# Attention scratch: sixteen heads' q and k scattered into a padded scratch and read back in two pieces

## The chip, the cores and the metric

One core of one Trainium2 chip runs the whole kernel. The metric is the device time of one execution in microseconds (us), the median of several runs.

## What is computed

The input `x` is (8, 256, 128) in float32: eight sequences of 256 tokens with 128 features. Two layers are applied, each the sum of an "attention" part and a "ffn" part on the normalised input:

```python
x = x + L0_attn(norm(x)) + L0_ffn(norm(x))
x = x + L1_attn(norm(x)) + L1_ffn(norm(x))
```

- `L0_attn` is an encoder block with 16 heads. The heads are cut by `reshape(B * 16, L, 8)`, without a transpose, so that head n of a sequence holds tokens 16 n to 16 n + 15, each with its 128 features seen as 16 rows of 8. `softmax(q k')` plus a relative position bias is multiplied by v; an output projection, a norm and a linear feed-forward follow.
- `L0_ffn` is a chain of six nodes, each with an 8-head attention of 16 features per head.
- `L1_attn` is a state space block (convolution, scan with 16 states, gated output) and a GELU feed-forward; `L1_ffn` routes each token to 2 of 8 experts.

## The kernel before, in words

The eight sequences are worked off one behind another in a software pipeline. Four lanes of stages (`CELL`, `SIDE`, `RAW`, `LAYER1`) exist for each sequence b; a table (`START`, `PLACES`) gives each stage of each engine a place, and every engine runs its stages in the order of these places, without reordering. So each engine is one queue in which work of up to three sequences is interleaved, and a stage that waits holds everything behind it on its engine. All DMAs are issued from one queue, that of SyncE (SP).

Attention B is the 8-head attention of the six nodes (groups 0 to 11 of four heads in each sequence); attention A is the 16-head one (groups 0 to 3). In both, q and k lie in strips of 32 partitions, four heads to a group: rows 0 to 15 (B) or 0 to 7 (A) of a strip are features, and row 16 (B) or 8 (A) holds -1 in k and the row maximum in q. A group goes through: `maximum` (L784, products q k' of the features alone), `tops` (L1307, row maxima on VectorE), `max_rows` (L792 transposes them on TensorE, ScalarE copies them at L1059, and SP sends them with a small DMA into the strips of q, L599), `score` (L802, the products again, now with the extra row, so that the maximum is subtracted), `exp` (L1066) and `values` (L815, L822).

For A, the projections give `qkv_a` (128 partitions, q, k and v of 256 tokens), with the features ordered so that a head must be gathered across tokens. That goes through a scratch in device memory:

- `a_write` (L566) writes q, k and v as they lie, 384 rows of 1 KB.
- `a_stack` (L585) reads the heads back with eight DMAs, one for q and one for k of each group. Each reads 4 heads x 512 rows in runs of 64 bytes, so that the strips come in with their 24 padding rows, for which the scratch has spare rows. It waits for `a_written` and for the last score of A of the sequence before.
- `v_read` (L592) reads v back in the same manner (16 heads x 128 rows of 64 bytes).
- `o_write`, `o_read` (L605, L611) take the attention's output back through a second scratch; L869 is the product that uses it.

In the SP queue, `a_write` and `a_stack` of sequence b stand ahead of `o_write` and of `rows B 10`, `o_read` and `rows B 11` of sequence b-1. For b = 0, 2 and 4 `a_stack` follows `a_write` at once; for the others `rows A 3` of the sequence before lies between them.

Of the kernel before, what the change touches and what calls it, by code (L numbers as in the profile page):

```python
# [7 lines left out]
F32 = mybir.dt.float32  # L8
# [173 lines left out]
def hybrid_layers(nc, t):  # L182

    ctx = ExitStack()
    with ctx:
        def sb(name, shape, dt=F32):
            return ctx.enter_context(nc.sbuf_tensor(name, shape, dt))
# [4 lines left out]
        def sig(name, per, step=1, sides=1):  # L192
            return Signal([one(f"{name}{i}" if sides > 1 else name) for i in range(sides)], per, step)
# [15 lines left out]
        rows = sb("rows", [P, t["rows"].shape[0], D])  # L209
# [35 lines left out]
        nt = sb("nt", [P, 2, NODES, L])  # L245
        qs = {"B": [sb(f"qs_b{i}", [P, 2, L]) for i in range(2)], "A": [sb(f"qs_a{i}", [P, L]) for i in range(A_GROUPS)]}
        ks = {"B": [sb(f"ks_b{i}", [P, 2, L]) for i in range(2)], "A": [sb(f"ks_a{i}", [P, L]) for i in range(A_GROUPS)]}
        qkv_a = sb("qkv_a", [P, 3, L])
# [108 lines left out]
        x_loaded = sig("x_loaded", 1, 16, 2)  # L357
        stacked_a = sig("stacked_a", 1, 2 * 4 * 16)
        maxed = {"B": [sig(f"maxed_B{i}", NODES, 16, 2) for i in range(2)], "A": [sig(f"maxed_A{i}", A_GROUPS // 2, 16) for i in range(2)]}
        a_written = sig("a_written", 1, 16)  # L360
        v_read = sig("v_read", 1, 16)
# [157 lines left out]
        def _(sp):  # L519
# [41 lines left out]
            def a_write(b):  # L561
                sp.wait_ge(*qkv_a_done.at(b, 1))
                hold(sp, s_held)
                past(sp, stacked_a, b - 1)
                past(sp, v_read, b - 1)
                sp.dma_start(bass.AP(tensor=a_scr.tensor, offset=0, ap=[[L, P], [A_PITCH * L, 3], [1, L]]), qkv_a[:, :, :]).then_inc(a_written.of(b), 16)  # L566
                if b == 0:
                    sp.wait_ge(s_memset, SETUP_POOL)
                    for first, n in A_SPARE:
                        sp.dma_start(a_scr[first:first + n, :], ks["A"][0][0:n, :]).then_inc(s_spare, 16)  # L570

            def gathered(i, first, heads, features):

                return bass.AP(tensor=a_scr.tensor, offset=i * A_PITCH * L + 16 * first, ap=[[16, heads], [L, 16 * features], [1, 16]])

            def a_stack(b):
                sp.wait_ge(*a_written.at(b))
                hold(sp, s_held)
                if b:
                    strips_ready(sp, b - 1, "score", "A", A_GROUPS - 1)  # L580
                else:
                    sp.wait_ge(s_spare, 16 * len(A_SPARE))
                for g in range(A_GROUPS):
                    for i, x in enumerate((qs["A"][g], ks["A"][g])):
                        sp.dma_start(x[:, :].rearrange("p (c r) -> p c r", c=CB), gathered(i, AG * g, AG, STRIP)).then_inc(stacked_a.of(b), 16)  # L585

            def v_read_(b):
                sp.wait_ge(*a_written.at(b))
                hold(sp, s_held)
                if b:  # L590
                    ready(sp, b - 1, "awo")
                sp.dma_start(va_hd[:, :].rearrange("p (c r) -> p c r", c=CB), gathered(2, 0, AH, AW)).then_inc(v_read.of(b), 16)  # L592

            def max_rows(b, kind, k):
                sp.wait_ge(*maxrow_done[kind].at(b, k))
                side, row = (b % 2, BW) if kind == "B" else (0, AW)
                x = qs["B"][side][:, k % 2, :] if kind == "B" else qs["A"][k][:, :]
                dst = bass.AP(tensor=x.tensor, offset=x.offset + row * x.ap[0][0], ap=[[STRIP * x.ap[0][0], 4], [1, L]])
                sp.dma_start(dst, maxrow[kind][side][k % 2][:, :]).then_inc(maxed[kind][k % 2].of(b), 16)  # L599
# [32 lines left out]
        def _(pe):  # L632
# [135 lines left out]

            def strip(tiles, b, kind, g, j, rows, first, n):
                part, span = slice(STRIP * j, STRIP * j + rows), slice(first, first + n)  # L770
                return tiles["B"][b % 2][part, g % 2, span] if kind == "B" else tiles["A"][g][part, span]

            def maximum(b, kind, g):
                if kind == "B":
                    pe.wait_ge(*k_done.at(b, g))
                    pe.wait_ge(*q_done.at(b, g))
                elif g == 0:
                    pe.wait_ge(*stacked_a.at(b))
                rows = BW if kind == "B" else AW
                take_strips(b, "max", kind, g)  # L780
                for qc in range(2):
                    for j in range(4):
                        o = strips[j // 2][:, (2 * (j % 2) + qc) * L:(2 * (j % 2) + qc + 1) * L]
                        mm = pe.matmul(o, strip(qs, b, kind, g, j, rows, qc * P, P), strip(ks, b, kind, g, j, rows, 0, L), start=True, stop=True)  # L784
                mm.then_inc(s_strips, 1)
# [9 lines left out]
            def score(b, kind, g):  # L795
                pe.wait_ge(*maxed[kind][g % 2].at(b, g // 2))
                rows = (BW if kind == "B" else AW) + 1
                take_strips(b, "score", kind, g)
                for kc in range(2):
                    for j in range(4):  # L800
                        o = strips[j // 2][:, (2 * (j % 2) + kc) * L:(2 * (j % 2) + kc + 1) * L]
                        mm = pe.matmul(o, strip(ks, b, kind, g, j, rows, kc * P, P), strip(qs, b, kind, g, j, rows, 0, L), start=True, stop=True)  # L802
                mm.then_inc(s_strips, 1)
# [745 lines left out]
        def _(pool):  # L1549
            pool.memset(half_neg[:, :], -0.5).then_inc(s_memset, 1)  # L1550
            pool.memset(vb[:, :, :, :, :], 0.0).then_inc(s_memset, 1)
            pool.memset(va[:, :, :, :], 0.0).then_inc(s_memset, 1)
            pool.memset(ks["A"][0][:, :], -1.0).then_inc(s_memset, 1)
            pool.memset(xi[:, :, :], 0.0).then_inc(s_memset, 1)
            pool.wait_ge(s_memset, 5)

# [82 lines left out]
SETUP_DVE = 3 * NODES + 2 * (NODES - 1) + 1 + 1 + 1 + 1 + 1 + CH + 2  # L1639
SETUP_POOL = 7  # L1640
T_BANK = (SETUP_DVE - 2) % 2
# [97 lines left out]
```

## Time and profile before

| | before |
|---|---|
| median of 3 runs | 1828.98 us (1828.89 to 1836.7) |
| profiled execution, its own time | 1828.94 us |
| its span, first to last instruction | 1827.1 us |
| busy: PE, DVE, ACT, POOL | 1384.5, 1066.4, 745.2, 271.6 us |
| mean granted TensorE clock | 0.808 |

PE is TensorE, DVE VectorE, ACT ScalarE, POOL GpSimd, and SPq the queue of SyncE. In a row of a timeline the first number is the start, the second the duration of the merged group, "xN" its count of instructions, and the bracket the engine's idle time just before it with what ended it. A float32 matmul is recorded as two instructions.

### The profile page before, as it was taken

How to read it: one execution, taken by the hardware profiler on the slowest of the kernel's cores; microseconds unless marked ns; L12 is line 12 of the kernel's file. 1: busy time of each engine (PE TensorE's matmuls, PEld its weight loads, DVE VectorE, ACT ScalarE, POOL GpSimd, SP SyncE). 2: the span in 40 equal slices, each digit the busy share in tenths (PEclk: the TensorE clock that was granted, in tenths of full speed). 3: DMA queues.
4: the chain of work that ended last, by engine and by line, in shares of the span. 5: the costliest groups of instructions: out<-in, count | busy, mean ns of one | idle time of the engine just before them, and what ended most of it. 6: DMA issues, size and time to landing. Idle time of an engine off the chain costs nothing.

```text
span 1827.1 us, 28722 instructions
## 1 busy us (share of the span) xinstructions
PE 1384.5 (76%) x10896; PEld 932.4 (51%) x10896; DVE 1066.4 (58%) x1757; ACT 745.2 (41%) x1420; POOL 271.6 (15%) x276
## 2 busy tenths in 40 slices
PE   6657866778598759876997959876987959778528
PEld 5434444445384437644664538544764538445407
DVE  2313323486368736784669536873668536875684
ACT  0223333455354534543455434542445434533323
POOL 0000001022111301031102201130102201121070
PEclk9667787779798879888897779867897779868858
DMA  4061021001210032002210131002110131001201
GB/s 154 23 62 12 2 29 16 1 13 21 45 62 4 22 53 56 13 13 35 57 39 13 17 49 62 5 21 35 48 39 12 18 48 59 4 13 42 83 1 61
DMA packets 199511, 62.20 MB, mean 34 GB/s; under 512 B 169232, under 2 KB 181296, under 8 KB 199248
## 3 DMA queue, kind: packets, MB, share of 16 engines
q1 hardware_dynamic: 199376, 60.36, 15.2%
q8 instruction: 90, 1.47, 0.3%
q14 instruction: 45, 0.37, 0.1%
HBM read 54.02 MB, written 5.80 MB: 33 GB/s over the span
## 4 chain that ended last, share of the span: by engine, by line
PE 51%; DVE 18%; SPq 14%; issue 7%; ACT 6%; DMA 3%; POOL 1%; DVEq 0%; ACTq 0%; POOLq 0%
SPq L585 12%; PE strips L802 9%; PE attn_out L815 7%; PE ps L963 6%; PE ps L975 5%; PE strips L784 5%; DVE hb L1448 4%; DVE rowmax_B L1307 3%; ACT probs L1066 3%; DVE hb L1443 2%; PE ps L740 2%; PE ps L644 2%; DVE rowmax_A L1307 2%; DVE work L1417 1%; PE attn_out L822 1%
## 5 line engine op out<-in xcount | busy, mean ns | idle before, releaser
L1066 ACT ACTIVATE probs<-strips 128x1024 f32<-128x1024 f32 x256 | 248.9, 1021 | 298.7 <-PE strips L802 298.0
L802 PE MATMUL strips<-qs_b,ks_b 17*128 17x256 f32 x1536 | 157.9, 541 | 203.6 <-DMA qs_b<-maxrow_B 139.8
L1307 DVE TENSOR_REDUCE rowmax_B<-strips 128x4 f32<-128x1024 f32 x192 | 227.2, 1219 | 136.0 <-PE strips L784 136.0
L802 PEld LDWEIGHTS strips<-qs_b,ks_b 17*128 17x128 f32 x1536 | 98.4, 255 | 241.7 <-DMA qs_b<-maxrow_B 142.3
L1448 DVE TENSOR_TENSOR_SCAN hb<-da,hb 128x1024 f32<-128x1024 f32 x64 | 149.2, 2331 | 2.2
L784 PE MATMUL strips<-ks_b,qs_b 16*128 16x256 f32 x1536 | 130.5, 460 | 22.8 <-ACT probs L1066 12.0
L815 PE MATMUL attn_out<-probs,vb 128*32 128x256 f32 x1536 | 142.2, 512 | 1.4 <-ACT probs L1066 1.4
L1534 DVE SCALAR_TENSOR_TENSOR work<-hb,ps 128x512 f32<-128x512 f32 x128 | 86.6, 686 | 96.2 <-ACT hb L1192 95.7
L975 PE MATMUL ps<-ze,w_e 128*128 128x256 f32 x512 | 127.2, 386 | 2.9 <-DVE work L1534 1.8
L963 PE MATMUL ps<-w_e,work 128*128 128x128 f32 x1024 | 125.1, 277 | 1.2 <-DVE work L1534 1.2
L963 PEld LDWEIGHTS ps<-w_e,work 128*128 128x128 f32 x1024 | 121.1, 192 | 8.2 <-DVE work L1534 4.5
L1153 ACT ACTIVATE da<-gate,a_neg 128x255 f32<-128x255 f32 x256 | 108.0, 496 | 21.0 <-DVE hb L1448 16.9
L784 PEld LDWEIGHTS strips<-ks_b,qs_b 16*128 16x128 f32 x1536 | 81.8, 216 | 64.7 <-issue 40.6
L1192 ACT ACTIVATE hb<-ps 128x512 f32<-128x512 f32 x128 | 75.5, 597 | 88.0 <-PE ps L975 85.9
L1618 POOL TENSOR_TENSOR cv_t<-hb 128x512 f32<-128x512 f32 x56 | 71.0, 1268 | 265.8 <-DVE hb L1452 265.8
L1074 ACT ACTIVATE out_sb<-attn_out 128x512 f32<-128x512 f32 x80 | 47.8, 597 | 148.7 <-PE attn_out L822 85.6
L975 PEld LDWEIGHTS ps<-ze,w_e 128*128 128x128 f32 x512 | 91.6, 190 | 22.1 <-issue 8.3
L1443 DVE TENSOR_TENSOR hb<-ps,dtx 128x1024 f32<-128x1024 f32 x64 | 78.0, 1218 | 38.0 <-PE ps L918 31.1
L1334 DVE TENSOR_TENSOR rem_a<-ps,xn_bo 128x256 f32<-128x256 f32 x8 | 3.4, 425 | 157.3 <-PE ps L869 157.3
L918 PE MATMUL ps<-bc,sel 96*128 96x256 bf16 x256 | 53.0, 328 | 53.1 <-DVE hb L1452 21.2
L815 PEld LDWEIGHTS attn_out<-probs,vb 128*32 128x32 f32 x1536 | 51.0, 137 | 73.0 <-issue 54.9
L1307 DVE TENSOR_REDUCE rowmax_A<-strips 128x4 f32<-128x1024 f32 x64 | 75.9, 1219 | 13.9 <-PE strips L784 13.9
(259 smaller groups left out, 2263.4 us busy)
## 6 DMA issues: line engine op xcount, KB each, us to landing
w_e<-in_w_e SPq DMA_DIRECT2D x128, 256.0 KB, 3.1
qs_a<-a_scr SPq DMA_DIRECT2D x32, 128.0 KB
ks_a<-a_scr SPq DMA_DIRECT2D x32, 128.0 KB
a_scr<-qkv_a SPq DMA_DIRECT2D x8, 384.0 KB, 2.6
pos<-t_scr SPq DMA_DIRECT2D x8, 264.0 KB, 11.3
qs_b<-maxrow_B SPq DMA_DIRECT2D x96, 4.0 KB
probs<-in_b_we_t SPq DMA_DIRECT2D x1, 1280.0 KB, 7.2
x_in<-in_x SPq DMA_DIRECT2D x8, 128.0 KB, 3.0
```

The costliest lines, as they stand in the source:

```text
L585: sp.dma_start(x[:, :].rearrange("p (c r) -> p c r", c=CB), gathered(i, AG * g, AG, STRIP)).then_inc(stacked_a.of(b), 16)
L784: mm = pe.matmul(o, strip(qs, b, kind, g, j, rows, qc * P, P), strip(ks, b, kind, g, j, rows, 0, L), start=True, stop=True)
L802: mm = pe.matmul(o, strip(ks, b, kind, g, j, rows, kc * P, P), strip(qs, b, kind, g, j, rows, 0, L), start=True, stop=True)
L815: mm = pe.matmul(attn_out[32 * j:32 * j + 32, i * L:(i + 1) * L], v, heads[:, j, kc, :], start=(kc == 0), stop=(kc == 1))
L963: mm = pe.matmul(o[:, h * D:(h + 1) * D], eh[:, e % 2, j, h * P:(h + 1) * P], w_e2[:, (b * EX + e) % RING, j, :], start=(j == 0), stop=(j ...
L975: mm = pe.matmul(o[:, j * L:(j + 1) * L], w_e1[:, n % RING, f * P:(f + 1) * P], ze[:, :], start=True, stop=True)
L1066: act.activation(probs[:, group % 2, 2 * i:2 * i + 2, :, :].rearrange("p h a b -> p (h a b)"), strips[i][:, :], ACT.Exp).then_inc(s_exp, 1)
L1153: last = act.activation(da[:, k % 2, m, j, 1:L], dt[:, m, 1:L], ACT.Exp, scale=a_neg[:, m, 2 * k + j:2 * k + j + 1])
L1307: dve.tensor_reduce(out=rowmax[kind][:, b % sides_n, k % 2, 2 * i:2 * i + 2, :], in_=strips[i][:, :].rearrange("p (h q t) -> p h q t", h=2 ...
L1443: dve.tensor_tensor(hk, o, dtx[:, :, :].unsqueeze(2).to_broadcast([P, CH, 2, L]), ALU.mult).then_inc(hb_done.of(b), 1)
L1448: dve.tensor_tensor_scan(flat_h, flat_a, flat_h, 0.0, ALU.mult, ALU.add).then_inc(scan_done.of(b), 1)
L1534: dve.scalar_tensor_tensor(out=eh[:, e % 2, 2 * k:2 * k + 2, :], in0=eh_t[:, i % 2, :, :], scalar=1.0, in1=parts_of(bank(b, ("h", i)), 2), ...
```

## The change

The scratch is laid out as the strips are: 32 heads' strips (16 of q, 16 of k) of 32 rows. It is filled with zeros once, and the rows of -1 are put in once. Per sequence, q and k are each scattered by one DMA in runs of 64 bytes (128 partitions x 16 heads), v goes to a scratch of its own, and the strips come back with one DMA for q and one for k, 512 rows of 1 KB each. `qs["A"]` and `ks["A"]` become one tile each for all four groups. The products of the strips take all 32 rows in place of 8, 9, 16 or 17. The setup has two memsets in place of one, and the fills of the scratch.

```diff
-A_PITCH = P + 16
-A_SPARE = [(P, 16), (A_PITCH + P, 16), (2 * A_PITCH + P, P), (2 * A_PITCH + 2 * P, A_PITCH + 16 * STRIP - 2 * A_PITCH - 2 * P)]
...
-        qs = {"B": [sb(f"qs_b{i}", [P, 2, L]) for i in range(2)], "A": [sb(f"qs_a{i}", [P, L]) for i in range(A_GROUPS)]}
+        qs = {"B": [sb(f"qs_b{i}", [P, 2, L]) for i in range(2)], "A": sb("qs_a", [P, A_GROUPS, L])}
...
-        a_scr = nc.dram_tensor("a_scr", [A_PITCH + 16 * STRIP, L], F32).ap()
+        a_scr = nc.dram_tensor("a_scr", [2 * AH * STRIP, L], F32).ap()
+        v_scr = nc.dram_tensor("v_scr", [P, AH, 16], F32).ap()
...
+            sp.wait_ge(s_memset, SETUP_POOL)
+            for i in range(2):
+                dst = bass.AP(tensor=a_scr.tensor, offset=i * AH * STRIP * L, ap=[[L, P], [P * L, A_GROUPS], [1, L]])
+                sp.dma_start(dst, ks["A"][:, :, :]).then_inc(s_spare, 16)
...
-                sp.dma_start(bass.AP(tensor=a_scr.tensor, offset=0, ap=[[L, P], [A_PITCH * L, 3], [1, L]]), qkv_a[:, :, :]).then_inc(a_written.of(b), 16)
                 if b == 0:
-                    sp.wait_ge(s_memset, SETUP_POOL)
-                    for first, n in A_SPARE:
-                        sp.dma_start(a_scr[first:first + n, :], ks["A"][0][0:n, :]).then_inc(s_spare, 16)
-
-            def gathered(i, first, heads, features):
-
-                return bass.AP(tensor=a_scr.tensor, offset=i * A_PITCH * L + 16 * first, ap=[[16, heads], [L, 16 * features], [1, 16]])
+                    sp.wait_ge(s_spare, 32)
+                    sp.dma_start(bass.AP(tensor=a_scr.tensor, offset=(AH * STRIP + AW) * L, ap=[[STRIP * L, AH], [1, L]]), qs["A"][0:AH, 0, :]).then_inc(s_spare, 16)
+                for i in range(2):
+                    dst = bass.AP(tensor=a_scr.tensor, offset=i * AH * STRIP * L, ap=[[16, P], [STRIP * L, AH], [1, 16]])
+                    sp.dma_start(dst, qkv_a[:, i, :].rearrange("p (n r) -> p n r", n=AH)).then_inc(a_written.of(b), 16)
+                sp.dma_start(v_scr.rearrange("p n r -> p (n r)"), qkv_a[:, 2, :]).then_inc(a_written.of(b), 16)
...
-                for g in range(A_GROUPS):
-                    for i, x in enumerate((qs["A"][g], ks["A"][g])):
-                        sp.dma_start(x[:, :].rearrange("p (c r) -> p c r", c=CB), gathered(i, AG * g, AG, STRIP)).then_inc(stacked_a.of(b), 16)
+                for i, x in enumerate((qs["A"], ks["A"])):
+                    src = bass.AP(tensor=a_scr.tensor, offset=i * AH * STRIP * L, ap=[[L, P], [P * L, A_GROUPS], [1, L]])
+                    sp.dma_start(x[:, :, :], src).then_inc(stacked_a.of(b), 16)
...
-                sp.dma_start(va_hd[:, :].rearrange("p (c r) -> p c r", c=CB), gathered(2, 0, AH, AW)).then_inc(v_read.of(b), 16)
+                src = bass.AP(tensor=v_scr.tensor, offset=0, ap=[[16, AH], [AH * 16, AW * CB], [1, 16]])
+                sp.dma_start(va_hd[:, :].rearrange("p (c r) -> p c r", c=CB), src).then_inc(v_read.of(b), 16)
...
-            def strip(tiles, b, kind, g, j, rows, first, n):
-                part, span = slice(STRIP * j, STRIP * j + rows), slice(first, first + n)
+            def strip(tiles, b, kind, g, j, first, n):
+                part, span = slice(STRIP * j, STRIP * j + STRIP), slice(first, first + n)
...
-            pool.memset(ks["A"][0][:, :], -1.0).then_inc(s_memset, 1)
+            pool.memset(ks["A"][:, :, :], 0.0).then_inc(s_memset, 1)
+            pool.memset(qs["A"][0:AH, 0, :], -1.0).then_inc(s_memset, 1)
```

## Rows read from the trace of the kernel before

**Rows 1.** The page's part 4: the chain that ended last, by line.

```profile
SPq L585 12%; PE strips L802 9%; PE attn_out L815 7%; PE ps L963 6%; PE ps L975 5%; PE strips L784 5%; DVE hb L1448 4%; DVE rowmax_B L1307 3%; ACT probs L1066 3%; DVE hb L1443 2%; PE ps L740 2%; PE ps L644 2%; DVE rowmax_A L1307 2%; DVE work L1417 1%; PE attn_out L822 1%
```

**Rows 2.** The page's part 5: busy time, mean, idle before, releaser.

```profile
L802 PE MATMUL strips<-qs_b,ks_b 17*128 17x256 f32 x1536 | 157.9, 541 | 203.6 <-DMA qs_b<-maxrow_B 139.8
```

**Rows 3.** Timeline of the SP queue around `a_stack` of sequence 4.

```profile
832.75 0.38 SPq L566 DMA_DIRECT2D a_scr<-qkv_a  x1
...
836.40 3.69 SPq L585 DMA_DIRECT2D ks_a<-a_scr  x1
...
863.29 3.70 SPq L605 DMA_DIRECT2D o_scr<-out_hd  x1
...
868.01 0.55 SPq L599 DMA_DIRECT2D qs_b<-maxrow_B  x1
868.67 0.37 SPq L611 DMA_DIRECT2D va_hd<-o_scr  x1
869.09 1.48 SPq L599 DMA_DIRECT2D qs_b<-maxrow_B  x1
```

**Rows 4.** Timeline of PE in the same stretch.

```profile
844.89 0.38 PE L792 MATMUL ps<-ident,rowmax_B 128*4 128x128 f32 x2 [0.35 <-DVE rowmax_B L1307]
...
852.27 0.38 PE L792 MATMUL ps<-ident,rowmax_B 128*4 128x128 f32 x2
870.78 2.09 PE L802 MATMUL strips<-qs_b,ks_b 17*128 17x256 f32 x16 [18.13 <-DMA qs_b<-maxrow_B]
```

**Rows 5.** PE timeline: the first of the eight such waits, sequence 0.

```profile
121.26 2.09 PE L802 MATMUL strips<-qs_b,ks_b 17*128 17x256 f32 x16 [12.43 <-DMA qs_b<-maxrow_B]
```

**Rows 6.** Timeline of ACT: the output of A copied for `o_write`.

```profile
845.08 0.38 ACT L1093 ACTIVATE out_hd<-ps 128x256 f32<-128x256 f32 x1
```

**Rows 7.** The last sequence, which no `a_stack` follows: SP, then PE.

```profile
1654.65 0.33 SPq L605 DMA_DIRECT2D o_scr<-out_hd  x1
...
1656.71 0.37 SPq L611 DMA_DIRECT2D va_hd<-o_scr  x1
...
1661.46 2.09 PE L802 MATMUL strips<-qs_b,ks_b 17*128 17x256 f32 x16
```

**Rows 8.** DMA issues: size of one, median us from issue to landing.

```profile
a_scr<-qkv_a SPq DMA_DIRECT2D x8, 384.0 KB, 2.6
...
va_hd<-o_scr SPq DMA_DIRECT2D x8, 128.0 KB, 3.6
```

**Rows 9.** SP timeline: `a_write` of sequence 7.

```profile
1431.39 0.38 SPq L566 DMA_DIRECT2D a_scr<-qkv_a  x1
...
1449.94 0.55 SPq L585 DMA_DIRECT2D qs_a<-a_scr  x1
```

**Rows 10.** Line L802: matmul durations in ns, shortest, median, longest.

```profile
L802 PE MATMUL strips<-qs_b,ks_b x1536: 374/626/792, 82.8 to 1667.2; 17*128 17x256 f32 x192
...
L802 PE MATMUL strips<-qs_a,ks_a x512: 374/374/791, 168.7 to 1645.3; 9*128 9x256 f32 x171
```

**Rows 11.** PE by stretch: us, busy (instructions), granted clock, DMA share, GB/s.

```profile
871.00:874.00 3.00, 3.00 (x20) 0.50 0.69 192
```

**Rows 12.** PE timeline: the same work for sequence 3 and for sequence 4.

```profile
811.98 2.04 PE L822 MATMUL attn_out<-pos,va 128*32 128x256 f32 x16
...
832.79 0.60 PE L833 MATMUL ps<-ident,out_sb 128*128 128x128 f32 x4
...
1009.68 1.94 PE L822 MATMUL attn_out<-pos,va 128*32 128x256 f32 x16
...
1037.36 0.60 PE L833 MATMUL ps<-ident,out_sb 128*128 128x128 f32 x4
```

**Rows 13.** PE timeline: scores of B before and after the wait of rows 4.

```profile
821.08 1.15 PE L802 MATMUL strips<-qs_b,ks_b 17*128 17x256 f32 x16 [0.38 <-ACT probs L1066]
...
824.36 1.15 PE L802 MATMUL strips<-qs_b,ks_b 17*128 17x256 f32 x16 [1.14 <-ACT probs L1066]
...
875.02 2.09 PE L802 MATMUL strips<-qs_b,ks_b 17*128 17x256 f32 x16 [1.00 <-ACT probs L1066]
```

More of the change, by code:

```diff
@@ L245, in hybrid_layers @@
         nt = sb("nt", [P, 2, NODES, L])
-        qs = {"B": [sb(f"qs_b{i}", [P, 2, L]) for i in range(2)], "A": [sb(f"qs_a{i}", [P, L]) for i in range(A_GROUPS)]}
-        ks = {"B": [sb(f"ks_b{i}", [P, 2, L]) for i in range(2)], "A": [sb(f"ks_a{i}", [P, L]) for i in range(A_GROUPS)]}
+        qs = {"B": [sb(f"qs_b{i}", [P, 2, L]) for i in range(2)], "A": sb("qs_a", [P, A_GROUPS, L])}
+        ks = {"B": [sb(f"ks_b{i}", [P, 2, L]) for i in range(2)], "A": sb("ks_a", [P, A_GROUPS, L])}
         qkv_a = sb("qkv_a", [P, 3, L])
@@ L357, in hybrid_layers @@
         x_loaded = sig("x_loaded", 1, 16, 2)
-        stacked_a = sig("stacked_a", 1, 2 * 4 * 16)
+        stacked_a = sig("stacked_a", 1, 2 * 16)
         maxed = {"B": [sig(f"maxed_B{i}", NODES, 16, 2) for i in range(2)], "A": [sig(f"maxed_A{i}", A_GROUPS // 2, 16) for i in range(2)]}
-        a_written = sig("a_written", 1, 16)
+        a_written = sig("a_written", 1, 3 * 16)
         v_read = sig("v_read", 1, 16)
@@ L581, in a_stack @@
                 else:
[L582 to L585 removed]
+                    sp.wait_ge(s_spare, 48)
+                for i, x in enumerate((qs["A"], ks["A"])):
+                    src = bass.AP(tensor=a_scr.tensor, offset=i * AH * STRIP * L, ap=[[L, P], [P * L, A_GROUPS], [1, L]])
+                    sp.dma_start(x[:, :, :], src).then_inc(stacked_a.of(b), 16)
             def v_read_(b):
@@ L596, in max_rows @@
                 side, row = (b % 2, BW) if kind == "B" else (0, AW)
-                x = qs["B"][side][:, k % 2, :] if kind == "B" else qs["A"][k][:, :]
+                x = qs["B"][side][:, k % 2, :] if kind == "B" else qs["A"][:, k, :]
                 dst = bass.AP(tensor=x.tensor, offset=x.offset + row * x.ap[0][0], ap=[[STRIP * x.ap[0][0], 4], [1, L]])
@@ L767, in take_strips @@
                             pe.wait_ge(s_exp, EXP_AT[user, kind, g, i] + 1)
-            def strip(tiles, b, kind, g, j, rows, first, n):
-                part, span = slice(STRIP * j, STRIP * j + rows), slice(first, first + n)
-                return tiles["B"][b % 2][part, g % 2, span] if kind == "B" else tiles["A"][g][part, span]
+            def strip(tiles, b, kind, g, j, first, n):
+                part, span = slice(STRIP * j, STRIP * j + STRIP), slice(first, first + n)
+                return tiles["B"][b % 2][part, g % 2, span] if kind == "B" else tiles["A"][part, g, span]
             def maximum(b, kind, g):
@@ L778, in maximum @@
                     pe.wait_ge(*stacked_a.at(b))
-                rows = BW if kind == "B" else AW
                 take_strips(b, "max", kind, g)
@@ L783, in maximum @@
                         o = strips[j // 2][:, (2 * (j % 2) + qc) * L:(2 * (j % 2) + qc + 1) * L]
-                        mm = pe.matmul(o, strip(qs, b, kind, g, j, rows, qc * P, P), strip(ks, b, kind, g, j, rows, 0, L), start=True, stop=True)
+                        mm = pe.matmul(o, strip(qs, b, kind, g, j, qc * P, P), strip(ks, b, kind, g, j, 0, L), start=True, stop=True)
                 mm.then_inc(s_strips, 1)
@@ L796, in score @@
                 pe.wait_ge(*maxed[kind][g % 2].at(b, g // 2))
-                rows = (BW if kind == "B" else AW) + 1
                 take_strips(b, "score", kind, g)
@@ L801, in score @@
                         o = strips[j // 2][:, (2 * (j % 2) + kc) * L:(2 * (j % 2) + kc + 1) * L]
-                        mm = pe.matmul(o, strip(ks, b, kind, g, j, rows, kc * P, P), strip(qs, b, kind, g, j, rows, 0, L), start=True, stop=True)
+                        mm = pe.matmul(o, strip(ks, b, kind, g, j, kc * P, P), strip(qs, b, kind, g, j, 0, L), start=True, stop=True)
                 mm.then_inc(s_strips, 1)
@@ L1552, in _ @@
             pool.memset(va[:, :, :, :], 0.0).then_inc(s_memset, 1)
-            pool.memset(ks["A"][0][:, :], -1.0).then_inc(s_memset, 1)
+            pool.memset(ks["A"][:, :, :], 0.0).then_inc(s_memset, 1)
+            pool.memset(qs["A"][0:AH, 0, :], -1.0).then_inc(s_memset, 1)
             pool.memset(xi[:, :, :], 0.0).then_inc(s_memset, 1)
-            pool.wait_ge(s_memset, 5)
+            pool.wait_ge(s_memset, 6)
             pool.memset(vb[:, :, :, :, BW:BW + 1], 1.0).then_inc(s_memset, 1)
@@ L1639 @@
 SETUP_DVE = 3 * NODES + 2 * (NODES - 1) + 1 + 1 + 1 + 1 + 1 + CH + 2
-SETUP_POOL = 7
+SETUP_POOL = 8
 T_BANK = (SETUP_DVE - 2) % 2
```

## The prediction

> **What bounds the kernel now.** I read the page's chain of work first. Its largest single line is neither a product nor a reduction but line L585 in the SP queue, 12% of the span [rows 1], some 215 us: the issue of the eight gathers of `a_stack`. The second look is at the page's groups, for what TensorE pays for it: the scores L802 have 203.6 us of idle time ahead of them, 139.8 of it ended by the small DMA that brings the maxima, `qs_b<-maxrow_B` [rows 2]. That transfer is 4 KB; so the question is when it is issued.
>
> The timeline of SP answers it for one sequence, and seven others look alike. `a_write` is issued at 832.75. The first gather goes out freely (836.40 is the second), but each later one holds the queue for 3.7 to 3.9 us, and even `o_write` behind them has to wait for their descriptors (863.29, 3.70 us). Only at 868.01 is `rows B 10` issued [rows 3]. TensorE transposed those maxima at 844.89, ended its last other product at 852.27 + 0.38 = 852.65 and then stood still for 18.13 us [rows 4]. For sequence 0 the same wait is 12.43 us [rows 5]; the other six are between 17.6 and 18.6, and all eight sum to the 139.8 of [rows 2]. All engines are in-order queues coupled to TensorE, and DVE, ACT and POOL stand still in the same hole, so taking it away moves everything after it as a block.
>
> The last sequence is the control, since no `a_stack` follows it: `o_write` goes out in 0.33 us, `o_read` 2.06 us later, and the same score starts at 1661.46 without any wait for a DMA [rows 7].
>
> **What the change takes away.** Per sequence, eight gathers of 2048 pieces of 64 bytes. In place of 27.4 us of blocked SP (835.80 to 863.2) and 3.70 us in `o_write` come two reads of 512 pieces of 1 KB.
>
> **What it adds, and where it lies.** Two scatters of 2048 pieces of 64 bytes, from SBUF to device memory. The trace has no write in such small pieces. The nearest rows: a gather of as many pieces at 3.7 to 3.9 us; and `o_read`, also 2048 pieces of 64 bytes but with 128 partitions on one side and 16 or more blocks on the other, which was issued in 0.37 us, held the next issue for only 1.48 us [rows 3] and lands in 3.6 us in all [rows 8]. The scatter is like `o_read` in shape, so I take 1.5 us of throughput for each; the bounds are 0.4 us (nothing but the issue) and 3.9 us (as a gather). The Trainium skill explains the difference between the two rows: in "DMA: Bandwidth & Descriptors", section "Why a DMA increments its semaphore by 16 and not by 1", a DMA of this kind runs on the largest number of engines up to 16 that divides the slowest dimension of both sides. A gather has 4 heads there and would run on 4 engines, a scatter has 128 and would run on 16; by that rule a scatter costs an estimated 3.83 / 4 = 1.0 us. The same page's specifications say that pieces under 512 bytes cost a read-modify-write, which speaks against the change; no run here has shown it for a write, and even a doubled scatter stays under the bound of 3.9.
>
> In order, for sequence 4, all from 832.75: q out (0.4), k held behind it (1.5), v held (1.5), and the last of them lands some 2.6 us later [rows 8], so 838.8 against 835.8 before. Then the two reads: 1024 pieces of 1 KB; `a_write` moves 384 such pieces inside its 2.6 us, so at most 2.6 us for each, and they hold SP for 0.5 to 3 us. SP is free at 839.5 to 842. What waits next is `o_write`, which can't start before 845.08 + 0.38 = 845.46 [rows 6]: the scatters are hidden, with 3.5 us to spare. Then `o_write` 0.33, the weights 0.9, `rows B 10` at about 846.8, landed by 849.6 (the same transfer took 2.7 us, 868.01 to 870.7). TensorE needs it at 852.65. `o_read` goes out at 847.9 and lands at 851.5, before L869. So the cover from `a_write` to the point where TensorE would wait again is 852.65 - 2.7 - 1.3 - 832.75 = 15.9 us, and what has to fit in is 0.4 + 1.5 + 1.5 + 2.6 + 3 = 9 us, or 14 with both scatters at the bound. For sequences 1, 3, 5, 6 and 7 the write is issued 10 to 18.6 us ahead of `a_stack` [rows 9], and costs nothing at all. If the cover were gone, the score of B 10 would be late again, us by us.
>
> `a_stack` itself is needed much later (the first product of A in that sequence comes over 25 us later), and no wait for it shows in the trace. The fills of the scratch and the larger memsets fall into the setup, where SP and POOL have issued their own work early and then wait for the products of the weights: nothing. The write of -1 rows in sequence 0 takes the place of four fills: nothing.
>
> **All 32 rows.** A product over 9 rows and one over 17 have the same shortest duration, 374 ns [rows 10], and 16 recorded products take 1.15 us in both forms. So 32 rows of the same strip cost nothing; the unknown is whether they change the granted clock, which is a rival below.
>
> **The clock.** After the hole TensorE runs at a granted clock of 0.50, that is 1.2 GHz, until shortly before 883 [rows 11]: the score at 870.78 takes 2.09 us in place of 1.15. Two scores are 4.24 us apart there and 3.28 at the full clock of 2.4 GHz [rows 13]. Over the whole 11.9 us from 870.78 to the end of the next product L784 I count 11.3 us of products at the lower clock, some 6.6 at the full one; ScalarE's exponentials pace part of it, which leaves about 3 us. But the clock also falls in places without a hole: the same work takes 833.39 - 811.98 = 21.4 us in sequence 3 and 1037.96 - 1009.68 = 28.3 us in sequence 4 [rows 12], at the full and at the lower clock. So I can't say that the stretch after B 10 will always have the full one; I take half, 1.5 us for each of seven sequences (in sequence 0 the clock had fallen before the wait), 10.5 us, with bounds 0 and 21. And the 6.9 us of [rows 12] are paid in three sequences of six (4, 5, 6, by the distance of their waits, 204 to 205.5 us against 196 to 198 for 1 to 3). When everything moves, this is drawn anew: I keep the same number, with three more or three fewer as bounds, 21 us either way.
>
> **Sum.** 1827.1 - 139.8 - 10.5 = 1676.8 us of span. The profiled execution took 1828.94 against a span of 1827.1, 1.8 more, and the median of the runs is 1828.98, the same. That gives 1678.6, and I say 1677 us.
>
> **Rivals.**
>
> 1. *The holes go, and the clock rises too.* If full strips count as more work, or if TensorE without its holes keeps the full clock, all of the clock's terms come at once: 1677 - 10.5 - 21 = 1645, and less, about 1620, if the falls that all sequences share go too. For it: the falls lie in stretches of strip products, with their short waits. Against: with 8 and with 17 rows the clock has fallen alike. It decides if fewer than a third of the span's half-clock time is left.
> 2. *Part of the hole stays.* The scatters cost more than the bound, or the reads do. Each us beyond the 15.9 of cover costs 1 us in sequences 0, 2 and 4 first, and in the others beyond some 25 to 34. With scatters of 10 us each, 2 x 10 + 0.4 + 2.6 + 3 = 26, so 10 us of hole in up to three sequences: 1707. If the small writes went at a rate that leaves half of each hole, 1677 + 70 = 1747. For it: no row prices a small write to device memory. Against: every row with small pieces is under 4 us for 2048.
> 3. *The release is absorbed.* Another wait takes its place, VectorE's chain of the scans above all (L918 and L792 wait for it). DVE is busy 1066 of 1827 us, 58%, and would be 64% of 1677; and it is idle in the hole. If a quarter of the gain were lost so: 1677 + 38 = 1715.
> 4. *Slower.* One mechanism: the scatter to addresses 32 KB apart is so slow that `a_stack` waits for `a_written` longer than the gathers took. In sequences that issue the write right before it, this starts at 868.0 - 832.75 - 2.6 - 3 - 1.3 = 28 us for both, in the others at some 46. Over the kernel it takes about 20 us per scatter, five times the slowest row of as many pieces; then 1850 us.
>
> **How the numbers follow.** The likeliest course 0.80 (its own range 1645 to 1709, the two clock terms at their ends, 10.5 + 21 = 31.5 around 1677, rounded), rival 1 0.07, rivals 2 and 3 together 0.11, rival 4 0.02. A range of 1645 to 1709 holds all of the first and the mild part of 2; its ends are for both clock terms at once, so it isn't widened. This kernel's measurement can tell about 0.5% from no change. All cases but the last are faster by more than 4%: faster 0.97, same 0.01, slower 0.02.
>
> **What would show it.** In the profile after: line L585 out of the chain's first places; in SP's timeline two issues at L585 under 3 us together and `o_write` and `rows B 10` no later than 15 us after `a_write`; the idle time ahead of L802 that `qs_b<-maxrow_B` ends down from 139.8 to under 15 us; 16 strip products still in 1.15 us at the full clock; some 90 thousand fewer packets (each sequence trades 16384 small ones for 4096 small ones and 1024 of 1 KB); the period between the scores of B 10 about 18 to 25 us shorter. The prediction is wrong if a wait at L503 for `a_scr<-qkv_a` of more than 10 us appears, or if the hole reappears ahead of another line, or if the half-clock time doesn't stay within a third of what the stretches outside the holes have now.

## The result, and the profile after

The changed kernel takes 1611.42 us (median of four runs, 1609.6 to 1618.7); the ratio to the kernel before, measured beside it at 1832.84 us, is 0.8796, with a 95% interval of 0.8755 to 0.8836. It is faster by 12%. I had forecast 1677 us with a range of 1645 to 1709: the direction and the larger part are right, the time lies 34 us below the range. A second set of runs gave 1612.21 us and 0.8825 (0.8772 to 0.8878).

The page of the profile after: its first line, part 1's line of the matmuls, the granted clock in part 2, part 4's chain, and two groups of part 5.

```profile
span 1616.9 us, 28690 instructions
...
PE 1284.9 (79%) x10896; PEld 888.4 (55%) x10896; DVE 1067.4 (66%) x1757; ACT 743.6 (46%) x1420; POOL 272.7 (17%) x277
...
PEclk9777998889998999899998999899989998789659
...
PE strips L802 10%; PE strips L785 7%; PE ps L963 6%; PE ps L975 6%; PE attn_out L815 6%; DVE rowmax_B L1307 5%; ACT probs L1066 5%; DVE hb L1448 5%; DVE hb L1443 3%; PE ps L742 2%; PE attn_out L822 2%; DVE rowmax_A L1307 2%; PE ps L646 2%; DVE work L1417 2%; PE ps L793 1%
...
L802 PE MATMUL strips<-qs_b,ks_b 32*128 32x256 f32 x1536 | 129.6, 457 | 75.3 <-ACT probs L1066 45.8
...
L785 PE MATMUL strips<-ks_b,qs_b 32*128 32x256 f32 x1536 | 114.2, 412 | 23.1 <-ACT probs L1066 12.4
```

SP's line, the first in [rows 1], is gone from the chain. The idle time ahead of the scores fell from 203.6 us to 75.3. The 139.8 us that the maxima's transfer ended [rows 2] are all gone, and the rest rose from 63.8 to 75.3 us, most of it waits for ScalarE. But there is a second change that these waits do not explain: TensorE, with the same 10896 matmuls, is busy 1284.9 us in place of 1384.5. The number of products is the same and they are 100 us shorter, those whose form did not change too: the 1536 of L815 on `probs` and `vb` went from 142.2 to 111.9 us.

```profile
L815 PE MATMUL attn_out<-probs,vb 128*32 128x256 f32 x1536 | 142.2, 512 | 1.4 <-ACT probs L1066 1.4
...
L815 PE MATMUL attn_out<-probs,vb 128*32 128x256 f32 x1536 | 111.9, 419 | 9.2 <-ACT probs L1066 9.2
```

The first of these lines is from the kernel before, the second from the changed one. So the products ran at a higher clock. The mean granted clock went from 0.808 to 0.905:

```profile
core 0: 1616.9 us, clock 0.905
```

The granted clock has two levels here, 0.5 and 1 of 2.4 GHz, so 2 x (1 - mean) x span is the time at the lower one, with TensorE busy or not: before 2 x 0.192 x 1827.1 = 702 us, after 2 x 0.095 x 1616.9 = 307.

SP's queue for sequence 2, the counterpart of [rows 3]:

```profile
391.19 1.33 SPq L574 DMA_DIRECT2D a_scr<-qkv_a  x2
392.57 1.85 SPq L575 DMA_DIRECT2D v_scr<-qkv_a  x1
397.27 0.36 SPq L586 DMA_DIRECT2D qs_a<-a_scr  x1
397.67 0.51 SPq L586 DMA_DIRECT2D ks_a<-a_scr  x1
404.00 0.33 SPq L607 DMA_DIRECT2D o_scr<-out_hd  x1
...
405.35 0.52 SPq L601 DMA_DIRECT2D qs_b<-maxrow_B  x1
```

From the first scatter to `rows B 10` it is 14.2 us; before it was 35.3. (For sequence 4 itself it is 15.6 us, 739.72 to 755.30.) Between the last read and `o_write` SP is idle for 5.8 us: it is now waiting for data, and nobody for it. TensorE at the place of [rows 4], sequence 3 to 4:

```profile
759.25 0.38 PE L793 MATMUL ps<-ident,rowmax_B 128*4 128x128 f32 x2
759.60 1.15 PE L802 MATMUL strips<-qs_b,ks_b 32*128 32x256 f32 x16
...
762.89 1.15 PE L802 MATMUL strips<-qs_b,ks_b 32*128 32x256 f32 x16 [1.50 <-ACT probs L1066]
```

No bracket at 759.60: the score follows the transpose at once, and takes 1.15 us, at the full clock, where it waited 18.13 us and took 2.09. The distance to the next is 3.29 us, as [rows 13] had it for the full clock.

### The profile page after: what moved, and what is told of

It is laid out like the page before. It is cut to its first block, busy times and chain, and to the rows that moved or that the text cites. A ratio compares the mean times of both kernels' runs of the same rounds, so it can differ in the third digit from the quotient of the medians.

```text
span 1616.9 us, 28690 instructions
## 1 busy us (share of the span) xinstructions
PE 1284.9 (79%) x10896; PEld 888.4 (55%) x10896; DVE 1067.4 (66%) x1757; ACT 743.6 (46%) x1420; POOL 272.7 (17%) x277
## 4 chain that ended last, share of the span: by engine, by line
PE 56%; DVE 22%; issue 10%; ACT 9%; DMA 2%; POOL 1%; SPq 0%; DVEq 0%; ACTq 0%; POOLq 0%
PE strips L802 10%; PE strips L785 7%; PE ps L963 6%; PE ps L975 6%; PE attn_out L815 6%; DVE rowmax_B L1307 5%; ACT probs L1066 5%; DVE hb L1448 5%; DVE hb L1443 3%; PE ps L742 2%; PE attn_out L822 2%; DVE rowmax_A L1307 2%; PE ps L646 2%; DVE work L1417 2%; PE ps L793 1%
## 5 line engine op out<-in xcount | busy, mean ns | idle before, releaser
L802 PE MATMUL strips<-qs_b,ks_b 32*128 32x256 f32 x1536 | 129.6, 457 | 75.3 <-ACT probs L1066 45.8
L802 PEld LDWEIGHTS strips<-qs_b,ks_b 32*128 32x128 f32 x1536 | 83.3, 213 | 106.4 <-issue 103.4
L785 PE MATMUL strips<-ks_b,qs_b 32*128 32x256 f32 x1536 | 114.2, 412 | 23.1 <-ACT probs L1066 12.4
L815 PE MATMUL attn_out<-probs,vb 128*32 128x256 f32 x1536 | 111.9, 419 | 9.2 <-ACT probs L1066 9.2
L785 PEld LDWEIGHTS strips<-ks_b,qs_b 32*128 32x128 f32 x1536 | 72.3, 189 | 58.3 <-issue 36.4
L918 PE MATMUL ps<-bc,sel 96*128 96x256 bf16 x256 | 51.2, 319 | 55.1 <-DVE hb L1452 21.4
L1621 POOL TENSOR_TENSOR cv<-cv,cv_t 128x512 f32<-128x512 f32 x56 | 82.3, 1470 | 4.4
L1452 DVE TENSOR_TENSOR hb<-hb,ps 128x1024 f32<-128x1024 f32 x64 | 78.1, 1221 | 2.2
```

The costliest lines, as they stand in the source:

```text
L785: mm = pe.matmul(o, strip(qs, b, kind, g, j, qc * P, P), strip(ks, b, kind, g, j, 0, L), start=True, stop=True)
L802: mm = pe.matmul(o, strip(ks, b, kind, g, j, kc * P, P), strip(qs, b, kind, g, j, 0, L), start=True, stop=True)
L815: mm = pe.matmul(attn_out[32 * j:32 * j + 32, i * L:(i + 1) * L], v, heads[:, j, kc, :], start=(kc == 0), stop=(kc == 1))
L1621: pool.tensor_tensor(ysum[:, :, :], ysum[:, :, :], pair[:, :, :], ALU.add).then_inc(ysum_done.of(b), 1)
```

## The experiments

The question after the result: the waits account for 139.8 us of the 210 us between the two profiled spans (1827.1 and 1616.9). Where do the other 70 come from? Theory R: from the number of rows that a strip product uses, which I had priced at nothing. Theory H, the rival: from the holes themselves, which let the clock fall, and whose absence lets it stay up; the rows do nothing. Each kernel was compared with the kernel before on its own chip, so the ratios are the safer comparison between groups; within a group the medians can be set side by side.

### The scratch's part alone

```diff
-                part, span = slice(STRIP * j, STRIP * j + STRIP), slice(first, first + n)
+                part, span = slice(STRIP * j, STRIP * j + rows), slice(first, first + n)
...
+                rows = BW if kind == "B" else AW
...
+                rows = (BW if kind == "B" else AW) + 1
```

> The changed kernel with the products of the strips over 8, 9, 16 and 17 rows again, so that only the scratch's part of the change is left. Theory R (the number of rows that a product uses is what keeps the granted clock up): the waits of 139.8 us are gone but the clock falls as before; 1677 us as predicted for the scratch, between 1660 and 1700, mean granted clock about 0.81 to 0.84, half-clock time over 500 us. Theory H (the clock rises because TensorE has no holes any more, the rows cost and bring nothing): 1611 us like the changed kernel, within 8 us, clock 0.905.

Measured: 1666.56 us (1657.87 to 1682.08), ratio 0.9164 (0.9085 to 0.9243), which is 1676 us for the 1828.98 of my forecast. The time is what theory R said. The profiled execution is the fastest of the four; its clock in slices, and the group of the scores:

```profile
PEclk9766877677998799979997799879987999779759
...
L804 PE MATMUL strips<-qs_b,ks_b 17*128 17x256 f32 x1536 | 135.9, 476 | 73.1 <-ACT probs L1068 43.1
```

The idle time is that of the changed kernel (73.1 against 75.3 us); the products take 135.9 us against 129.6, and the mean clock is 0.854, 2 x 0.146 x 1656.1 = 484 us at the lower level. That is a higher clock than the 0.81 to 0.84 that I had expected for theory R; the other three executions have 0.836 to 0.846. H is out as the whole cause, but it holds a part: TensorE is busy 1345.3 us here, so 39 of the 100 us of shorter products came with the holes' end, without full rows, and 60 with the rows. Not all of that is time: between this span and that of the changed kernel lie 39.2 us, because TensorE's idle time rose by 21 us (310.8 to 332.0) while its products took 60 less.

### The rows alone, holes kept

The kernel before, with B's products over 32 rows and A's over 8 and 9 (in its layout A's strips hold other data in the rows beyond).

```diff
-                rows = BW if kind == "B" else AW
+                rows = STRIP if kind == "B" else AW
...
-                rows = (BW if kind == "B" else AW) + 1
+                rows = STRIP if kind == "B" else AW + 1
```

> The kernel before with the products of attention B over all 32 rows (A stays at 8 and 9), the eight gathers untouched. Theory R: the waits for the maxima stay at about 140 us, but the clock outside them rises; 1829 - 50 = about 1780 us (1765 to 1800), clock above 0.84. Theory H: 1829 us, within 8 us, clock 0.81.

> The kernel before with B's products over 32 rows, once more, for a trace of an undisturbed execution beside the others. 0.98 of the time before, about 1790 us; the idle time ahead of the scores that the maxima's transfer ends is still 139 to 142 us, and the half-clock time is down from 705 us by 60 to 110 us.

Measured: 1789.53 us, 0.9802 (0.973 to 0.9873), and in the second set 1783.87 us, 0.9784 (0.9712 to 0.9856), so about 2%, or 35 to 40 us by the medians, from B's rows alone. Both intervals exclude 1. The trace read here is that of the second set.

```profile
L802 PE MATMUL strips<-qs_b,ks_b 32*128 32x256 f32 x1536 | 142.4, 495 | 211.8 <-DMA qs_b<-maxrow_B 142.3
```

The waits are all there (142.3 us), and the clock is 0.844 all the same: 2 x 0.156 x 1788.7 = 558 us at the lower level, 144 less than before, more than the 60 to 110 I had written down. TensorE is busy 1331.1 us, 53 less than before, and 38 of them reach the span (1788.7). The rows act without any change to the scratch.

### 24 rows

```diff
-                rows = BW if kind == "B" else AW
+                rows = 24
```

> The changed kernel with all products of the strips over 24 rows. If the rows count by their number (theory R, by degrees): between the changed kernel and the one over few rows, about 1625 to 1655 us. If a product counts only with its strip full (theory R, all or nothing): about 1677 us. Theory H: 1611 us, as 32 rows.

Measured: 1650.22 us (1640.61 to 1655.49), 0.904 (0.8978 to 0.9102), clock 0.874. On the same chip the few rows gave 1666.56, and the two sets don't overlap. 32 rows gave 0.8796 and 0.8825. So it goes by degrees: 24 rows bring some of it (16 us by the medians, 23 by the ratios), the last eight the larger part (39 us by the ratios). The clock of the four executions is 0.857 to 0.874, where few rows have 0.836 to 0.854 and 32 rows 0.905 to 0.912.

### The holes put back

Behind the two reads, eight gathers in the old form into a tile that nothing reads; the next `a_write` waits for them.

```diff
+                for n in range(8):
+                    src = bass.AP(tensor=a_scr.tensor, offset=16 * AG * (n % A_GROUPS), ap=[[16, AG], [L, 16 * STRIP], [1, 16]])
+                    sp.dma_start(idle_in[:, n, :].rearrange("p (c r) -> p c r", c=CB), src).then_inc(idle_read.of(b), 16)
```

> The changed kernel with eight gathers of 2048 pieces of 64 bytes each put back behind the two reads of the strips, into a tile that nothing uses: the hole is back, the full rows stay. Theory R: 1611 + 140 to 150 for the waits + some 20 for the cold start after each = 1765 to 1785 us. Theory H: all of the gain is lost, 1825 to 1835 us. The idle time ahead of the scores that the transfer of the maxima ends is 140 to 165 us in both.

Measured: 1801.95 us (1797.28 to 1813.31), 0.9887 (0.9818 to 0.9956).

```profile
L809 PE MATMUL strips<-qs_b,ks_b 32*128 32x256 f32 x1536 | 137.9, 482 | 245.5 <-DMA qs_b<-maxrow_B 175.0
```

More than I expected, because the holes are longer than the old ones: 175.0 us in place of the 140 to 165 that I wrote down. The eight gathers now come on top of the two scatters and the two reads, and SP issues `rows B 10` of sequence 3 41.3 us after the write (821.78 to 863.03), where it was 35.3. With this length theory R's sum is 1611 + 175 + 20 = 1806 us, and theory H's is 1829 + 35 = 1864: R is within 4 us of the measured time. Set against the kernel before, it is the other half of the test. By the ratio this kernel takes 1808 us, 21 less than the kernel before although its holes are 35 us longer, so the full rows are worth 56 us (give or take 13 by the interval) with the holes in place, about what they are worth without them.

Between the two spans lie 1797.1 - 1616.9 = 180.2 us, and 175.0 of them are the idle time itself. What eight holes cost beyond their own length is then 5 us in this pair of executions, 1801.95 - 1612.21 - 175.0 = 15 us by the medians, and 19 by the ratios (194 - 175), with some 16 either way by the intervals. The cold start is a small term, 0.7 to 2.4 us for each hole, and the runs can't tell it well from nothing.

### Are the scatters hidden?

The changed kernel again as the base, and each scatter issued three times and eight times, the additional ones into scratch that nothing reads.

```diff
+                for i in range(14):
+                    dst = bass.AP(tensor=more_scr.tensor, offset=i * AH * STRIP * L, ap=[[16, P], [STRIP * L, AH], [1, 16]])
+                    sp.dma_start(dst, qkv_a[:, i % 2, :].rearrange("p (n r) -> p n r", n=AH)).then_inc(a_written.of(b), 16)
```

> The changed kernel as it is, beside the other three on one chip: 1611 us, between 1600 and 1620, by both theories. It is the base for the differences below.

> The changed kernel with each scatter of q and k issued three times, the extra ones into scratch that nothing reads (four more scatters of 2048 pieces per sequence). Theory hidden (the scatters lie under the products of the sequence before, with some 8 to 10 us of cover left): within 4 us of the changed kernel. Theory exposed (a scatter is paid where it stands, about 1.6 us each): 8 x 4 x 1.6 = 50 us more.

> The changed kernel with each scatter issued eight times (fourteen more per sequence, about 22 us of transfer). Theory hidden, with a cover of 15.9 us from the write to the point where the maxima are missed and 6 to 9 us used: the holes come back, some 13 to 15 us in sequences 0, 2 and 4 and up to 8 in the others, 40 to 90 us over the changed kernel with the cold starts, 1650 to 1700 us. Theory exposed: 8 x 14 x 1.6 = 180 us more, 1790 us.

Measured: 1612.21 us (1609.93 to 1615.71) for the base; 1615.63 (1614.43 to 1618.22) with three times; 1741.65 (1732.94 to 1744.04) with eight. Thirty-two more scatters, four for each sequence, cost 3.4 us together, about the spread of the runs, so one pair is hidden well. With eight times, SP's queue around the write of sequence 2, then TensorE at two places:

```profile
415.60 1.39 SPq L575 DMA_DIRECT2D a_scr<-qkv_a  x2
417.03 22.34 SPq L578 DMA_DIRECT2D more_scr<-qkv_a  x14
439.41 1.69 SPq L579 DMA_DIRECT2D v_scr<-qkv_a  x1
...
444.54 0.43 SPq L611 DMA_DIRECT2D o_scr<-out_hd  x1
...
446.00 0.51 SPq L605 DMA_DIRECT2D qs_b<-maxrow_B  x1
```

```profile
450.41 2.09 PE L806 MATMUL strips<-qs_b,ks_b 32*128 32x256 f32 x16 [14.91 <-DMA qs_b<-maxrow_B]
...
624.91 2.09 PE L806 MATMUL strips<-qs_a,ks_a 32*128 32x256 f32 x16 [14.10 <-DMA qs_a<-maxrow_A]
```

A scatter moves in 22.34 / 14 = 1.60 us. In sequences 0, 2 and 4 the holes came back, 10.72, 14.91 and 14.59 us: the latter two as worked out (13 to 15), the first less. SP is free for `o_write` 28.9 us after the write (415.60 to 444.54), and 14.91 of them are paid, so the cover is 14.0 us. But the other five had not the "up to 8" of my expectation: there the `rows A 3` of the sequence before stands between `a_write` and `a_stack`, and its transfer was held, 74.1 us in all at the scores of A. Their cover is the distance to `rows A 3`, about 11 us (in sequence 3 it is issued 25.2 us after the write, and 14.10 of them are paid), and not that to `a_stack`. So the total was 129 us over the base and not 40 to 90.

### Whose rows matter

In both the tiles, the DMAs and the waits are those of the changed kernel. The edit of the first is shown; the second has A and B exchanged.

```diff
-                rows = BW if kind == "B" else AW
+                rows = STRIP if kind == "B" else AW
```

> The changed kernel with B's products over 32 rows and A's over 8 and 9. Theory R (rows keep the clock up, each product by its own rows): A has a quarter of the strip products but starts from fewer rows; between the changed kernel and the one with all products small, nearer the first: 1611 + a third of 55 = about 1630 us. A theory in which any strip over all of its 32 rows is enough nearby: 1611 us.

> The changed kernel with A's products over 32 rows and B's over 16 and 17. B full and A small took 22 us more than both full; both small took 55 us more (on another chip). If each product's own rows count, A full alone is worth the rest of that, so 1612 + 33 = about 1645 us, 1638 to 1655. If the two only work together: 1665 us.

Measured: B full and A small 1633.9 us (1632.56 to 1635.79), 0.8943 (0.8891 to 0.8996), on the base's chip, 22 us over it. A full and B small 1668.15 us (1663.54 to 1675.69), 0.9165 (0.9105 to 0.9225): not the 1645 of a sum, but just the time of few rows everywhere (0.9164). A's rows bring 22 us where B's are full, and nothing that can be seen where they are not (0.9164 and 0.9165, the difference known to about 0.01, or 18 us; the medians of the two sets are 1666.56 and 1668.15). B's rows bring 0.9164 - 0.8943, or 40 us, with A's small. So the gain does not look like a sum over the products, though with one set of runs for each kernel the interval only just excludes it, and only one trace of each was taken.

### Can more of it be had?

Two tries: five products of 128 rows in the longest wait that is left, and 32 zero rows more for the bfloat16 products that spread B and C of the scan.

```diff
+                if kind == "B" and g == 6:
+                    user, _, _, of = STRIP_LIST[at - 1]
+                    o = take(user, ("rows", "A", of))
+                    for i in range(5):
+                        pe.matmul(o[:, 0:L], ident[:, :], nt[:, b % 2, 0, :], start=True, stop=True)
...
-        bc3 = sb("bc3", [96, L], BF16)
+        bc3 = sb("bc3", [P, L], BF16)
```

> The changed kernel with five products of 128 rows and 256 columns that nothing reads, issued in the longest wait that every sequence still has (3.8 us, score B 6 for the row maxima of A 1), into the bank that is taken next. After that wait the clock falls for some 10 us in every sequence. If the clock follows what TensorE does in the wait: up to 8 x 4 = 30 us less, 1580 to 1605 us. If the bank comes free so late that the five run into the score: no gain or up to 15 us more, 1612 to 1627 us.

> The changed kernel with the products that spread B and C of the scan (bfloat16, 96 rows) over 128 rows, the last 32 all zero. If zero rows count for the clock in any product as they do in the strips: these are 51 us busy and a quarter wider would be worth little, 1600 to 1612 us. If only the strip form profits: 1612 us, within 4.

Measured: 1612.25 us (1609.7 to 1612.64) and 1611.12 us (1607.16 to 1612.28); neither is different from the changed kernel, and nothing came of the up to 30 us that I had hoped for from the first. The first moved the clock (0.918) and not the time. TensorE in that kernel, at the five products and behind them (the second line is the score behind the wait):

```profile
489.93 2.40 PE L803 MATMUL ps<-nt,ident 128*128 128x256 f32 x10 [1.57 <-DVE ctx_a L1334]
492.25 1.15 PE L808 MATMUL strips<-qs_b,ks_b 32*128 32x256 f32 x16
...
498.53 1.28 PE L924 MATMUL ps<-bc,sel 96*128 96x256 bf16 x6 [2.36 <-ACT qkv_a L1020]
499.74 2.09 PE L808 MATMUL strips<-qs_b,ks_b 32*128 32x256 f32 x16
```

The score at 492.25 now runs at the full clock (1.15 us; in the changed kernel the one at 496.99 took 1.90), and the time that it saves is waited out a little later for other engines; then the clock falls there, so that the next score takes 2.09 us. No version here beats the changed kernel.

## Why the prediction was right in one part and wrong in another

**What bounded the kernel** was read rightly. The chain's first line, the idle time ahead of L802, the order of SP's queue and the last sequence as a control gave 139.8 us for the waits, and all eight are gone. For the scratch's part the sum was 1677 us, and the kernel with that part alone has 0.9164 of the time before, 1676 us (1662 to 1691 by the interval). That the two agree to 1 us is in part luck. Its four executions span 1658 to 1682 us, and in the only one with a trace the clock's term was at its lower end (below).

**The scatters.** I took 1.5 us for each from the row of `o_read`, and it is 1.60; the bounds 0.4 and 3.9 held it. `a_written` is complete 6.1 us after the first scatter is issued (391.19 to 397.27), where I had 6.0. The two reads hold SP for 0.9 us, where I had up to 3. The cover was 14.0 us in sequence 2 where I had 15.9. One step was wrong without harm: from 384 pieces in 2.6 us I concluded that a read of 512 pieces takes at most 2.6, and the two land after 3.8 and 4.9 us (medians of eight). "Costs nothing at all" for the others is right at this size, but the reason overlooked the `rows A 3` behind the write. The rule of the Trainium skill in "DMA: Bandwidth & Descriptors", section "Why a DMA increments its semaphore by 16 and not by 1", put a scatter at 1.0 us by the ratio of engines; the order of the two forms is as it says, the size is 1.60. The same page's read-modify-write for pieces under 512 bytes is not to be seen as a cost of writing over reading: `o_read`, which reads 2048 pieces of 64 bytes, held the issue behind it until 1.48 us were over, and a scatter, which writes as many, takes 1.60 us. What either would take in larger pieces of the same total was not run.

**The clock after a hole.** I took 10.5 us with bounds of 0 and 21, 1.5 us a sequence. The ratio of the kernel with the scratch's part alone gives 1828.98 x 0.0836 = 152.9 us (138 to 167), of which 139.8 are waits: 13 us for both clock terms together, and anything from -1 to 28 within the interval. The eight holes put back give 5 to 19. The traces give it more directly. Between the products L869 of sequences 1, 2 and 3 lie 197.8 and 197.7 us before, 179.3 and 179.5 without their holes of 18.45 and 18.13; with few rows and no holes it is 177.1 and 177.3. So a hole cost 2.2 us beyond its length there, within the bounds of 0 to 3.

**The step that failed** is "So 32 rows of the same strip cost nothing". It took two things for one: how long a product takes at a given clock, and what clock it is granted. The first is as I said: the shortest duration of the strip products is 374 ns with 32 rows too, and 16 recorded products take 1.15 us.

```profile
L802 PE MATMUL strips<-qs_b,ks_b x1536: 374/374/792, 83.2 to 1456.4; 32*128 32x256 f32 x192
```

The second is to be read in the means and not in the shortest: a score's product of B takes 541 ns on average before, 476 with the scratch's part alone, and 457 with 32 rows. (The median went from 626 ns [rows 10] to 374, but that is the holes' doing: it is 374 with 17 rows too once they are gone.) This second question I put into rival 1 with a chance of 0.07, and set its price into no end of the range: the sum holds nothing for it. It is worth, with all rows full, 1666.56 - 1612.21 = 54 us by the medians and (0.9164 - 0.8825) x 1828.98 = 62 us by the ratios; 1677 less 62 is 1615. Between the two profiled executions it is 39.2 us, the least, since the one with few rows is the fastest of its four and the changed one the slowest. Of these, 16.0 us lie ahead of the first product L869 (258.70 and 242.66), 8.6 between it and the second, and 3.2 in each of the five distances that follow: over half of the gain falls into the first two sequences.

**Rival 1** named the mechanism, but I put 1645, with 1620 at the outside, and set as its mark that less than a third of the time at the lower clock is left; 307 of 702 us are left, 44%, and the time is 1611. So that mark would have let the rival pass as refuted. The prediction's last sign of being wrong did show: before, 116 of the 702 us at the lower clock lay inside the eight holes and 586 outside, and 307 is 48% less than that, not within a third. The argument against the rival, that the clock had fallen alike with 8 and with 17 rows, was no evidence about 32: both are small, and the trace had no strip product over more. Where a change takes a quantity to a value that the trace has nowhere, the trace excludes nothing, and the range should have held both ends.

**The lottery of the clock** in [rows 12] is one, and its term came out at its lower end. I had carried 21 us either way: three sequences of six that pay 6.9 us. With few rows and no holes the same stretch, from L822 to the end of L833, takes 21.4 us in all of sequences 1 to 6, so none pays. The span of 1676.8 less 21 is 1655.8 us, and that execution has 1656.1. (This too is closer than the terms are: up to the L869 of sequence 1 the gain was 8 us less than the holes' length, and the last distance, which held no hole, was 8 us shorter.) With A's rows full and B's few, five of the six take 25.3 to 27.2 us; with 24 rows, two of the six take 25.8. TensorE in the stretch of sequence 5 with few rows, and of sequence 4 with only A's full:

```profile
1104.70:1126.10 21.40, 17.67 (x202) 0.97 0.14 20
...
923.70:950.90 27.20, 25.36 (x202) 0.64 0.11 16
```

In the changed kernel the stretch of sequence 3 takes 719.06 to 740.36, 21.3 us, and the mean granted clock in it is full:

```profile
719.00:740.40 21.40, 17.69 (x206) 1.00 0.01 2
```

So the changed kernel alone does not show that the rows keep the fall away, since it is away in the trace with few rows too. What the runs add is this: in the nine traces of kernels with all of B's rows full (among them the holes put back, and B full in the kernel before) the stretch takes 21.3 to 21.5 us in all 54 cases. Wherever it was seen to take longer, B's products had 24 rows or fewer. Between the products L869 of sequences 1 to 6 lie 173.6 to 174.4 us, where before the distances were 197.7 and 197.8 for two of them and 204.2 to 205.5 for three; with few rows and no holes they are 177.1 to 178.1.

Where the clock still falls can be read side by side (the columns are the stretch, its length, TensorE's busy time and instructions, the granted clock, and the DMAs' share and GB/s). The kernel with few rows:

```profile
736.00:742.00 6.00, 4.80 (x30) 0.50 0.27 81
742.00:748.00 6.00, 4.81 (x40) 0.50 0.03 10
748.00:754.00 6.00, 5.72 (x56) 0.75 0.00 1
```

The changed kernel, some 29 us earlier in its own time, at the same work:

```profile
706.00:712.00 6.00, 2.86 (x24) 0.74 0.08 24
712.00:718.00 6.00, 4.55 (x40) 0.69 0.19 67
718.00:724.00 6.00, 5.20 (x63) 1.00 0.00 1
```

Both fall around the same wait of TensorE for VectorE, 2.93 us long in either, which ends at 735.69 with few rows and at 707.02 in the changed kernel. With few rows the lower clock is granted from 734.0 to 751.0, 17 us, through the strip products that follow; with full ones from 708.9 to 715.7, 7 us, over a second wait of 2.13 us and the products up to L793.

**The other rivals.** No part of the hole stayed, and the kernel is not slower. Something of the release was absorbed: over the whole span TensorE's idle time fell by 111 us (442.6 to 332.0), not by 139.8, so 29 us of other waits came in, 8 with the scratch's part alone and 21 with the rows. The waits for VectorE that every sequence has did not grow: 3.77 to 3.88 us ahead of one score in sequences 2 to 7, where they were 3.77 to 3.85 before.

**What stays open.** Why 24 rows bring a part, why the last eight bring more, and why A's rows seem to count only beside B's, is not settled; the runs show that the granted clock follows the rows, and not by what rule. With few rows the same kernel's executions lie 24 us apart and its traces differ in where the clock falls, so one trace is one draw. Nor was it tried whether the rows of the stationary or those of the moving operand do it.

## What to carry to other kernels

A queue that issues DMAs is a resource like an engine: read what stands behind each long issue, and weigh a chain of small pieces by who is held by it. If a product over few rows of the array lies in stretches with short waits, padding it with zero rows up to its full strip can be worth more than it looks, since its duration at a given clock does not change but the granted clock may. And when a change moves a quantity to where the trace has no row, put both signs of its effect on the clock into the range, however free the work looks at fixed clock.

## What the runs showed of the hardware

- The granted clock depends on the rows that products use, even if the added rows hold zeros in both operands, as rows 17 to 31 of B's strips do: over the executions of a kernel its mean is 0.836 to 0.854 with 8 to 17 rows, 0.857 to 0.874 with 24, and 0.905 to 0.912 with 32, all else being equal. Alone in the kernel before, B's rows gave 0.844 to 0.860 in place of 0.800 to 0.822.
- That effect does not look additive: A full alone 0.9165 of the time before, as much as none (0.9164); B full alone 0.8943; both 0.8825.
- A shorter product is not all time won: with full rows TensorE was busy 60 us less and idle 21 us more, and 39 us reached the span.
- A higher mean clock is not a shorter time by itself: filling a wait with products raised it (0.905 to 0.912 without, 0.918 to 0.921 with them), and the time stayed at 1612 us.
- A DMA that writes 2048 pieces of 64 bytes to device memory, with 128 as the outermost step on both sides, took 1.60 us; gathers of as many pieces with 4 heads as the outermost step held the queue for 3.7 to 3.9 us each.
